# Adaptive layer norm block on one core: probabilities of tiles 3 and 4 turned by a trip over DRAM, scores two tiles ahead from step 1, two small reorderings

## The reference

```python
mod = (silu(c) @ wmod).reshape(4, 6, 1, 512)      # sa, ca, ga, sb, cb, gb, one set for each batch
ga, gb = sign(ga) * max(|ga|, 0.25), sign(gb) * max(|gb|, 0.25)
h = layernorm(x) * (1 + ca) + sa
q, k = h @ Wq.T, h @ Wk.T                          # rank 64, the same for all 16 heads
attn = softmax(16-head scores: q @ k.T)            # every head has the same scores
x = x + ga * ((attn @ (h @ Wv.T)) @ Wo.T)
h = layernorm(x) * (1 + cb) + sb
x = x + gb * (einsum('btd,rde->bte', h, factors) / sqrt(8) + bias)
```

## Time and profile before

| | busy us | share of the span |
|---|---|---|
| span | 447.8 | |
| PE (TensorE) | 439.6 | 98% |
| PEld (weight loads) | 361.6 | 81% |
| DVE (VectorE) | 356.6 | 80% |
| ACT (ScalarE) | 320.0 | 71% |
| POOL (GpSimd) | 234.9 | 52% |

### The profile page before, as it was taken

The page is one execution under the profiler, slowest core; times in us unless marked ns, Lnnn a source line. Parts: engine busy times, 40 slices in busy tenths (PEclk is TensorE's granted clock), DMA queues, the critical chain, the costliest instruction groups (busy, mean ns, idle before and its releaser), DMA issues.

```text
span 447.8 us, 7294 instructions
## 1 busy us (share of the span) xinstructions
PE 439.6 (98%) x2118; PEld 361.6 (81%) x2118; DVE 356.6 (80%) x610; ACT 320.0 (71%) x642; POOL 234.9 (52%) x308
## 2 busy tenths in 40 slices
PE   8899999999999999999999999999999999999996
PEld 7586888878888888788888888888888888887885
DVE  5787557868887887988897878888886777999977
ACT  3677557778797786678877787779777664667651
POOL 0554516852555643356565544456564527177982
PEclk9999999999999999999999999999999999999999
DMA  8999986533665457667676367766686146658423
GB/s 308 393 388 287 256 156 115 120 121 108 204 210 184 133 159 217 205 210 235 209 243 201 117 200 221 234 187 215 187 254 198 47 140 203 200 172 278 131 79 141
DMA packets 77750, 88.05 MB, mean 197 GB/s; under 512 B 5000, under 2 KB 55944, under 8 KB 77200
## 3 DMA queue, kind: packets, MB, share of 16 engines
q1 hardware_dynamic: 73872, 80.51, 56.4%
q0 software_dynamic: 3264, 6.29, 7.9%
q10 hardware_dynamic: 576, 0.79, 0.5%
HBM read 53.49 MB, written 34.10 MB: 196 GB/s over the span
## 4 chain that ended last, share of the span: by engine, by line
PE 77%; DVE 9%; issue 4%; POOL 3%; ACT 3%; DMA 3%; SPq 0%; DVEq 0%; POOLq 0%; ACTq 0%
PE ps_o L525 9%; PE ps_o L527 9%; PE ps_o L526 9%; PE ps_v L525 5%; PE ps_v L526 5%; PE ps_v L527 5%; PE ps_y L525 4%; PE ps_y L527 4%; PE ps_y L526 4%; PE ps_qk L525 3%; PE ps_qk L526 3%; PE ps_qk L527 3%; PE ps_s L614 2%; PE ps_s L615 2%; PE ps_t L531 1%
## 5 line engine op out<-in xcount | busy, mean ns | idle before, releaser
L1685 POOL TENSOR_SCALAR ve<-mv 128x1 f32<-128x1 f32 x64 | 17.0, 266 | 160.0 <-DVE mv L1320 119.3
L525 PE MATMUL ps_o<-v_lo,pt_hi 128*128 128x512 f32 x192 | 74.9, 390 | 1.0 <-DVE pt_lo L1205 0.9
L526 PE MATMUL ps_o<-v_hi,pt_lo 128*128 128x512 f32 x192 | 74.8, 389 | 0.0
L527 PE MATMUL ps_o<-v_hi,pt_hi 128*128 128x512 f32 x192 | 74.8, 389 | 0.0
L1205 DVE TENSOR_TENSOR h_lo<-h_f,h_hi 128x512 fp32r<-128x512 f32 x57 | 41.6, 730 | 29.0 <-ACT h_hi L843 28.7
L871 ACT ACTIVATE h_f<-x1b,mod_t 128x128 f32<-128x128 f32 x120 | 52.9, 594 | 3.8 <-DVE x1b L1338 3.8
L1687 POOL TENSOR_TENSOR rstd<-ve,minus_half 128x1 f32<-128x1 f32 x64 | 45.8, 716 | 5.3
L525 PEld LDWEIGHTS ps_o<-v_lo,pt_hi 128*128 128x128 f32 x192 | 36.0, 188 | 9.3 <-issue 1.8
L525 PE MATMUL ps_v<-wvo_lo,h_hi 128*128 128x512 f32 x108 | 43.1, 399 | 0.3 <-DVE h_lo L1205 0.3
L919 ACT ACTIVATE probs<-ps_s,negmax 128x1024 f32<-128x1024 f32 x32 | 35.4, 1108 | 10.0 <-DVE negmax L1264 9.7
L526 PE MATMUL ps_v<-wvo_hi,h_lo 128*128 128x512 f32 x108 | 42.2, 391 | 0.0
(11 more groups left out here) (238 smaller groups left out, 1193.2 us busy)
## 6 DMA issues: line engine op xcount, KB each, us to landing
x_blocks<-xn SPq DMA_DIRECT2D x50, 256.0 KB, 2.8
p_blocks<-probs SPq DMA_DIRECT2D x24, 512.0 KB, 3.8
pb<-p_blocks SPq DMA_DIRECT2D x96, 128.0 KB, 2.7
x1b<-x_blocks SPq DMA_DIRECT2D x30, 256.0 KB, 2.8
result<-x_ring SPq DMA_DIRECT2D x15, 512.0 KB, 3.0
xb<-x_blocks SPq DMA_DIRECT2D x20, 256.0 KB, 3.0
x_ring<-in_x SPq DMA_DIRECT2D x18, 256.0 KB, 4.0
wmod<-in_wmod SPq DMA_DIRECT2D x4, 1024.0 KB, 14.9
```

What stands on the lines that cost most here:

```text
L525: nc.tensor.matmul(acc, a_hi, b_lo, start=first, stop=False)
L526: nc.tensor.matmul(acc, a_lo, b_hi, start=False, stop=False)
L527: return nc.tensor.matmul(acc, a_hi, b_hi, start=False, stop=last)
L1685: nc.gpsimd.tensor_scalar(ve[:, one], mv[:, u, 1:2], EPS, None, ALU.add).then_inc(ve_done, 1)
```

## The change

It has four parts.

1. `LAST_EARLY` is 2 and no longer 4. Tiles 3 and 4 are no longer turned by TensorE but go over DRAM. Steps 0 makes the scores of tile 1, step 1 those of tile 2 and at its end those of tile 3; step 2 makes those of tile 4, step 3 those of tile 5. The queries of pair 2 (tiles 4 and 5) are copied at the end of step 1, no longer of step 2.
2. In VectorE's prologue the two parts of tile 0's h stand ahead of the moments of tile 2 and of the first `wvo_rest`.
3. On GpSimd `of_x(12)` stands between the second and the third of the four `f_lo` pieces, no longer behind the fourth.
4. The loop over the four pieces becomes the function `factor_rest`.

```diff
-LAST_EARLY = 4
+LAST_EARLY = 2
...
             nc.vector.tensor_copy(wqk_hi[:], wqk_raw[:]).then_inc(wqk_hi_done, 1)
+            h_first(0)
+            h_second(0)
             moments_of(2)
-            h_first(0)
             wvo_rest(0)
-            h_second(0)
             wvo_rest(1)
...
+            def factor_rest(k):
+                pool.wait_ge(f_hi_done, k + 1)
+                nc.gpsimd.tensor_tensor(f_lo[:, k, :], f_sum[:, k, :], full(f_hi[:, k, :]),
+                                        ALU.subtract).then_inc(f_lo_done, 1)
...
             pool.wait_ge(bias_loaded, 16)
-            for k in range(C):
-                pool.wait_ge(f_hi_done, k + 1)
-                nc.gpsimd.tensor_tensor(f_lo[:, k, :], f_sum[:, k, :], full(f_hi[:, k, :]),
-                                        ALU.subtract).then_inc(f_lo_done, 1)
+            factor_rest(0)
+            factor_rest(1)
             of_x(TB + 4, 0)
+            factor_rest(2)
+            factor_rest(3)
             of_x1(2, 0)
```

## The result

The changed kernel takes 450.81 us (median of 20 runs, 450.20 to 453.03); the kernel before, on the same chip, 449.65 (median of 20, 448.62 to 452.26). The ratio is 1.003, 95% interval 1.0015 to 1.0044: 1.2 us slower, as forecast (450.8). The profiled execution took 450.76 us, with a span of 449.0.

A forecast was written before the change was run, and what follows sets the result against it. The prediction took TensorE, busy 439.6 of 447.8 us, to bound the kernel. Adding +0.7 (part 2) and +0.5 (part 1) to 449.63 gave 450.8 us, forecast range 449.7 to 452.2, bounds of the terms 448.3 and 451.8.

The forecast's parts named there:

- What bounds the kernel: Whole kernel: TensorE is busy 439.6 of 447.8 us; waiting elsewhere costs nothing until it reaches TensorE.
- From 101 us on TensorE never waits, so what it has lost or won by then it keeps.: After 101 us: no TensorE waits, so the whole effect is decided ahead of attend(4).
- Part 2, +0.7: VectorE's prologue: the reordering makes tile 1's h_lo later, a loss of 0.7 us, bounds -0.2 and +0.9.
- the meeting that was priced: Prologue: tile 0's h_lo on VectorE meets GpSimd's wqk_lo, priced by v_lo's 1.40 us in place of 0.69.
- Part 1, step 2: Step 2: query copies meet GpSimd's additions; TensorE waits 0.9 and 1.7 us, and the step loses 2.6 us.
- Part 1, step 3: Step 3: attend(3) starts at 102.7 instead of 101.05, 1.65 us lost before step 4's 0.87 of transposes goes.
- a wait of 0.1 to 0.6: Ahead of feed_forward(0): TensorE waits 0.1 to 0.6 us for f_lo, covered by 0.7 us ahead of attend(3).
- The trip: Tiles 3 and 4 over DRAM: hidden, by 0.65 us plus another 0.7 for tile 3, 2 us for tile 4.
- late-trip rival: Tile 3's trip at the longest landings arrives at 97.0, 1.9 us more: 452.7 us; chance 0.14.
- The sum: Whole kernel: +0.7 for the prologue and +0.5 for steps 2 and 3 on 449.63 give 450.8 us.
- The upper bound of +1.3: Part 1, steps 2 and 3: the most it could lose, 1.3 us, used in the upper total of 451.8.
- The small gain: Rival: query copies slip past GpSimd, h_lo too: 448.3 us, to 449.6 with one of two meetings; chance 0.22.

The follow-up runs named there:

- e5: The change without parts 2 and 3, query copies behind tile 3's row maximum, tile 2's first pt_hi and tile 11's h_f ahead of tile 3's exponentials; 447.58 us, ratio 0.9970.
- e9: The changed kernel run once more, unaltered, on another call; 450.85 us, ratio 1.0047 to the kernel before.
- e8: The change with ScalarE's first pt_hi of tile 2 and h_f of tile 11 put ahead of tile 3's exponentials; 448.81 us, ratio 0.9985.
- e1: The kernel before with part 2 alone (the new VectorE order in the prologue); 449.77 us, ratio 1.0009.
- e11: e5 with part 2 (the change's new prologue order) put back; 448.78 us, ratio 0.9990 to the kernel before.
- e12: e5 unaltered, run again in another group; 447.22 us, ratio 0.9945 to the kernel before.
- e7: The change with part 3 undone, all four f_lo pieces ahead of of_x(12); 449.83 us, ratio 1.0029 to the kernel before.
- e2: The kernel before with part 1 alone (LAST_EARLY 2); 449.41 us, ratio 1.0002.
- e3: The change with part 2 undone, parts 1 and 3 kept; 449.74 us, ratio 1.0009 to the kernel before.
- e0: The kernel before, unaltered, run for a second trace; 449.54 us (8 runs).
- e10: The change with VectorE's copies of pair 2's queries moved behind tile 3's row maximum, second run; 448.30 us, ratio 0.9985 to the kernel before.

## Why the prediction was right, point by point

- **What bounds the kernel.** Right: in 11 of 13 traces the time from the last scores to the end is 45.0 to 45.2 us, so what TensorE had lost or won by then it kept; e5 and e9 have 0.7 more there, and why isn't known.
- **"From 101 us on TensorE never waits, so what it has lost or won by then it keeps."** Wrong. The profiled execution of before loses 1.5 us between s11 and s13, 1.1 of it in three gaps of 0.3 to 0.45 us, of which the list of waits has one (0.29 ahead of the values at 184.59), behind a VectorE wait of 2.04 us for a DMA. I looked at TensorE's list only. The term left out is -0.7 to -1.5 us.
- **Part 2, +0.7.** Direction and place right; measured 1.1 in the prologue. The wait moved from 20.84 to the queries and keys of pair 0, as said (0.65 us). What failed is "the change reorders this chain and takes nothing out of it", and with it the meeting that was priced. In the change the chain gets 1.0 us longer: 0.65 us of idling for ScalarE's `h_f`, which the sum had at nothing, and 0.2 by the rounding `h_hi` (0.81 to 1.01), while `h_lo` ("takes over 1.2 us") took 0.69. The trace could mislead here. In the first trace of before `v_lo` took 1.40 us, and just this delay let `h_f`, ready at 17.84, be there when VectorE was through with `wqk_hi`; so that trace shows no wait to be had. In e8, which begins the same way, all is as forecast: no idling, `h_lo` at 1.67, and 0.72 us lost. So the mechanism and its price hold for an execution like the one that was read, and not for the other six traces with the new order, where the idle time takes its place; that the price is near 1.1 there too is luck. The median of e1 (+0.3) is under the forecast, that of e11 against e12 (+1.56) over it.
- **Part 1, step 2.** Right in chain and nearly in size. Forecast: second copy ends 1.45 after the first, wait 0.9 ahead of tile 4's scores, 1.7 inside `attend(2)`. Measured: 1.29; 0.88 from start to start (the matmul at 86.04 would have been followed at 86.27; it was at 87.15), and 1.09 for `pt_lo`, the matmul before it having been at 91.02. Step 2 loses 2.4 us against 2.6 (`attend(1)` ends at 81.30 and `attend(2)` at 95.19: 13.89, against 10.61 before and 0.91 for a set of scores).
- **Part 1, step 3.** `attend(3)` was forecast for 102.7 plus the 0.7 of part 2. It starts at 103.89, less the 0.64 by which this trace's M is later: 103.25, 0.15 off. But it starts right behind tile 5's scores (103.62), so TensorE and VectorE arrive together, where I had TensorE waiting 0.7.
- **Part 3, "a wait of 0.1 to 0.6", "covered".** The wait is there (0.54 listed). Since there is no slack of 0.7 behind it, it isn't covered: 0.5 us by e7 against the change. On the old prologue it shows no cost (e2, e3), since a wait of 0.45 for `ffn`, which the prediction didn't have, goes with it.
- **The trip.** Right: hidden, the late-trip rival fell. Tile 3's block transpose runs at 95.45 without a wait, 1.0 later than reckoned (part 2 and this trace's later start would make 1.3). It is hidden only because the rest is late: in the faster variants VectorE waits for it, up to 1.65 us.
- **The skill's rule.** The Trainium skill, "SBUF — State Buffer", section "Who interferes with whom", says that a VectorE instruction with two SBUF inputs and a GpSimd one reading SBUF shut each other out. I had built part 2 on that sentence, so on `h_lo`. The same section says that copies and casts with one SBUF input can take the shared ports too, and that a reduction never does. The trace agrees with both: the casts `h_hi` and `qs_lo` were held up (1.01 in place of 0.41 us, 1.28 in place of 0.29), as was `h_lo` in e8 (1.67 in place of 0.69); the row maximum beside an addition was not (1.22). I should have asked of every VectorE instruction in the stretch, not of `h_lo` alone.
- **The sum.** +0.7 and +0.5 were to give 450.8. Measured by traces, the change (e9) against e0: +1.0 for the prologue, +0.95 for parts 1 and 3 up to s11, -0.8 from the late trips that stayed away. Part 1 by itself costs 0.84 to 0.94 up to s11 with the old prologue (e2 against before and e0) and 0.42 with the new one (e7 against e1). The upper bound of +1.3 for it was not derived in the sum. The total came out within 0.1 in the first comparison and 0.7 below the 1.9 us of the second, but the terms were larger, of both signs, and one was not on the list: that the number is so close is in good part luck. The small gain (448.3) is what e10 and e8 reach: 448.3 and 448.8, with the meeting or ScalarE's idle time taken off the path and not, as that rival had it, by chance.

## What to carry to other kernels

When work is moved forward on one engine, ask of each instruction moved when its inputs are ready, and of each one passed whether it filled a wait: twice here (`moments_of(2)` ahead of `h_first(0)`, ScalarE's `pt_hi` and `h_f` ahead of the exponentials) a piece of ready work set before a waiting one was worth 0.5 to 2 us. Put what nobody waits for yet (the query copies) behind what the next engine waits for (the row maximum), the more so where GpSimd holds up the first and not the second. Before taking a duration or the absence of a wait from one trace, look in a second one whether it is the rule: the 1.40 us of `v_lo`, on which part 2 was priced, stand in 2 of 13 traces. And before saying that nothing happens behind a point, compare two traces of the same kernel, mark by mark: TensorE's list of waits leaves out the short gaps, and of the 1.5 us lost there it had 0.3.

## What the runs showed of the hardware that I had not expected

- Of two short copies in a row on VectorE, beside queued additions of GpSimd, the second always lost too: 1.28 or 1.29 us in after, e2, e3, e7, e8 and e9, where it takes 0.29 alone. The first copy follows an addition, the next addition goes ahead of the second copy, though that stood ready on VectorE: in these six traces each side gets one turn. So two copies of 0.29 us cost 1.9 to 2.2.
- A wait of TensorE costs some 0.16 us more from start to start than is listed (0.72 listed, 0.88 paid; 0.93 and 1.09); the first matmul behind it also takes 0.47 to 0.50 in place of 0.39.
- A DMA of the same size at the same place of the program lands after 3.3 us (after) or 5.3 (before) for a store of 512 KB, and after 3.1 (after) or 4.7 (e0) for a load of 256 KB. The runs don't show why.
- A VectorE subtraction with both inputs in SBUF that meets one of GpSimd ends 0.55 or 0.56 us after it (1.40 in before, 1.61 and 1.67 in e8), a cast 0.14 or 0.15 (`qs_lo`) or 0.28 or 0.29 (`h_hi`) after.
